# Two-layer adaLN transformer in fp32: the stage between the two attentions is reordered, batch by batch

## The chip, the core and the metric

The kernel runs on one NeuronCore of a Trainium2 chip. The metric is the device time of one execution in microseconds (us). A core has five engines that each work through their own instruction stream in order and meet only at semaphores: TensorE (PE in the profile), VectorE (DVE), ScalarE (ACT), GpSimd (POOL), and SyncE (SP), which here issues all DMA transfers. TensorE writes to eight PSUM banks of 128 x 512 fp32; the other engines read them.

## What is computed

The input `x` is 2 batches of 512 rows of 512 columns, here 8 tiles of 128 rows, 4 for each batch. Cut to what matters, the reference is:

```
mod = (silu(c) @ wmod).reshape(2, 6, 1, 512)          # per layer: sa, ca, ga, sb, cb, gb
ga, gb = (2*(g >= 0) - 1) * maximum(abs(g), 0.25)      # clamped gates
x = x + ga * attention(layernorm(x) * (1 + ca) + sa)
x = x + gb * feed_forward(layernorm(x) * (1 + cb) + sb)
# layer 0: attention with 32 query heads, 8 key/value heads, window 128
#          feed-forward = h @ W.T + bias + sum_e w_e (h @ A_e.T) @ Bf_e.T
# layer 1: attention with latents: c_q = h @ Wq_down, c_kv = h @ Wkv_down (64 wide),
#          128 heads of 4 content columns and 64 rotary columns; then a mixture of LoRA experts
```

## The kernel before, in words

Products are made from split operands: a value is held as `_hi` plus `_lo` (both fp32r), and a group `mm3` of three matmuls per pair, `hi*hi + hi*lo + lo*hi`, stands for one fp32 product. Nothing is scheduled by a program: the order of each engine is the order in which its block of the source is written, and a wait holds everything behind it on that engine.

*Layer 0's attention* runs over 8 key/value heads (`kv_head`), each in two halves, one for each batch; a half has 4 slots, one for each block of 128 queries (`slot` 0 to 63; the last half is slots 60 to 63, batch 1 of head 7). In a slot, TensorE makes `scores`, DVE masks and reduces them (`mask`), ACT takes exponentials (`exps`), DVE divides (`normalise`), TensorE transposes (`transposes`) and multiplies with the values (`sum_values`), ACT and DVE split the result (`out_high`, `out_low`), and `project_out` adds the slot's share of the output, which `gate_attention` (DVE) gates and `add_attention` (POOL) adds to `x`. In all but the last half, TensorE fills the waits with the projections of the next half (`more` in the code).

*Between the attentions* stand, before the change all behind the last slot: the merge of layer 0's feed-forward weights (`merge(k)`: W.T plus the LoRA product, 4 groups of 6 fp32 matmuls, from transposed `fbfT` and scaled `fa_s`, split by `merged_high` on ACT and `merged_low` on DVE); layer 1's modulation (`mod(1, c)` for 6 chunks, `mod_use` turns each chunk's rows into columns or gate sums, `mod_cols`, `clamp_gates`, `broadcast_gate`); the second norm of layer 0 (`norm_stats`, `norm_rows` on DVE, transposes `norm` on TensorE, scale and shift on ACT into `full`, split into `hT_hi` and `hT_lo` by DVE and POOL in `norm_split` and `norm`); the feed-forward (`ffn(t)` for 8 tiles); the first norm of layer 1 (phase 2 of the same functions); and layer 1's latent stages: `latent` (both down-projections), the rotary keys (`kr_mm`, copied by ACT to `k1` and `km`, whose unused rows POOL has zeroed), `content(0)`, and the value columns `vc`. In the latent stages before, each function loops over both batches.

*Layer 1's attention* runs over 128 units (64 head pairs by 2 batches) in `period(u, ...)`. A period makes the scores of unit u, the row maxima of unit u+2 and the rotary queries of unit u+3 (`rope_queries`), so the first three periods (u = -3 to -1) only fill the pipeline, with `content(1)` to `content(3)` between them. The content parts go to DRAM and come back by DMA (`store_content`, then `km` and `q2`).

## Time and profile before

| | us |
|---|---|
| timed, 3 runs, median (lowest to highest) | 2375.38 (2375.05 to 2375.47) |
| profiled execution, its own time | 2367.75 |
| its span, first to last instruction | 2365.9 |
| mean granted TensorE clock over the span | 0.98 of full |

The profiled execution was 7.6 us shorter than the median of the timed ones. The table's span counts from the first instruction; every time of day in the rows is counted from there. The stage at stake lies between 719.68 (the last half of the first attention begins) and 898.14 (the scores of unit 0 of the second one).

### The profile page before, as it was taken

The page shows a single profiled execution, that of the slowest core. Times are in us where ns is not written, and L with a number is a line of the kernel's source. Part 1 is how long each engine was busy: PE and PEld are TensorE (multiplying, and loading weights), DVE is VectorE, ACT ScalarE, POOL GpSimd, SP SyncE. Part 2 cuts the span into 40 slices and gives each one's busy share as a digit, 9 for nine tenths or more (in the row PEclk, how much of TensorE's full clock was granted, in tenths as well). Part 3 has the DMA queues.
Part 4 walks back from the last instruction along what each step waited for, and adds up shares of the span by engine and source line. Part 5 has one row for each costly group of instructions (what it writes and reads, how often), then busy time and mean ns, then how long its engine had stood idle before and what let it go on. Part 6 is the DMA issues. An engine that isn't in the chain of part 4 may idle for free.

```text
span 2365.9 us, 40739 instructions
## 1 busy us (share of the span) xinstructions
PE 2254.3 (95%) x11084; PEld 1676.5 (71%) x11084; DVE 1661.0 (70%) x3066; ACT 1346.5 (57%) x2633; POOL 587.4 (25%) x428
## 2 busy tenths in 40 slices
PE   6999999999998879999999999999999999999968
PEld 4788888888885546777777777777777777776646
DVE  6677777787775557767676676767767676767746
ACT  2444444444543246767767676677767677676721
POOL 4455655655651320000000000000000000002322
PEclk9999999999998979999999999999999999999988
DMA  5101010100022132111111111111111111113330
GB/s 190 57 28 45 18 44 27 43 19 27 18 66 89 28 118 91 39 39 38 38 35 39 38 38 34 38 40 37 39 33 39 39 38 38 35 40 90 94 108 36
DMA packets 117151, 117.49 MB, mean 50 GB/s; under 512 B 28925, under 2 KB 71453, under 8 KB 117100
## 3 DMA queue, kind: packets, MB, share of 16 engines
q1 hardware_dynamic: 117100, 116.85, 16.4%
q8 instruction: 27, 0.44, 0.1%
q14 instruction: 24, 0.20, 0.0%
HBM read 95.30 MB, written 20.97 MB: 49 GB/s over the span
## 4 chain that ended last, share of the span: by engine, by line
PE 87%; DVE 7%; issue 2%; SPq 1%; DMA 1%; ACT 1%; POOL 1%; POOLq 0%; DVEq 0%; ACTq 0%
PE bank L1830 11%; PE bank L1817 11%; PE bank L1831 10%; PE bank L1842 10%; PE bank L1530 8%; PE bank L1532 8%; PE bank L1531 8%; PE bank L1805 5%; PE bank L1803 5%; PE bank L1804 5%; PE bank L1618 1%; DVE probs L1198 1%; DMA wm<-in_L_wmod 1%; DVE rope_b L1177 1%; DVE rope_a L1175 1%
## 5 line engine op out<-in xcount | busy, mean ns | idle before, releaser
L1379 DVE TENSOR_REDUCE mcol<-bank 128x1 fp32r<-128x512 f32 x1024 | 694.6, 689 | 375.6 <-PE bank L1817 370.2
L1817 PE MATMUL bank<-km,q 128*128 128x512 f32 x1024 | 422.2, 413 | 12.0 <-DVE mcol L1379 7.3
L1830 PE MATMUL bank<-q,k 128*128 128x512 f32 x1024 | 419.9, 410 | 6.7 <-DVE c_lo L1350 3.3
L1831 PE MATMUL bank<-q,k 128*128 128x512 f32 x1024 | 405.4, 396 | 0.0
L724 POOL TENSOR_TENSOR wr_lo<-wst,wr_hi 128x512 fp32r<-128x512 f32 x64 | 81.7, 1277 | 1231.5 <-DVE wr_hi L1338 1231.5
L1817 PEld LDWEIGHTS bank<-km,q 128*128 128x128 f32 x1024 | 316.9, 310 | 78.1 <-issue 20.9
L1019 ACT ACTIVATE x<-bank 128x512 f32<-128x512 f32 x512 | 285.3, 601 | 91.1 <-PE bank L1831 86.6
L1019 ACT ACTIVATE pT<-bank 128x512 f32<-128x512 f32 x512 | 285.1, 600 | 87.0 <-PE bank L1831 83.4
L1830 PEld LDWEIGHTS bank<-q,k 128*128 128x128 f32 x1024 | 195.6, 191 | 134.2 <-issue 117.9
L1831 PEld LDWEIGHTS bank<-q,k 128*128 128x128 f32 x1024 | 192.6, 188 | 37.0
L1805 PE MATMUL bank<-hT_hi,wr_lo 128*128 128x512 f32 x512 | 206.7, 404 | 0.0
L1803 PE MATMUL bank<-hT_hi,wr_hi 128*128 128x512 f32 x512 | 204.4, 399 | 0.7 <-ACT vc L984 0.7
L1804 PE MATMUL bank<-hT_lo,wr_hi 128*128 128x512 f32 x512 | 203.5, 397 | 0.0
L1015 ACT ACTIVATE ost<-bank 128x512 f32<-128x512 f32 x128 | 76.5, 598 | 182.7 <-PE bank L1842 182.7
L1530 PE MATMUL bank<-hT_hi,w_hi 128*128 128x512 f32 x384 | 156.9, 409 | 16.7 <-DVE rope_b L1177 10.1
L845 ACT ACTIVATE probs<-probs,nmax 128x256 f32<-128x256 f32 (+1 forms) x256 | 120.1, 471 | 76.3 <-DVE nmax L1187 76.3
L1532 PE MATMUL bank<-hT_hi,w_lo 128*128 128x512 f32 x384 | 153.4, 400 | 0.0
L1531 PE MATMUL bank<-hT_lo,w_hi 128*128 128x512 f32 x384 | 152.9, 398 | 0.0
L852 ACT ACTIVATE pT_hi<-bank 128x512 fp32r<-128x512 f32 x112 | 61.8, 596 | 142.4 <-PE bank L1618 142.4
L620 POOL TENSOR_TENSOR rope_a<-rope_a,rope_b 128x512 f32<-128x512 f32 x80 | 103.0, 1288 | 124.2 <-DVE rope_b L1177 124.2
L1842 PE MATMUL bank<-x,vp 128*32 128x512 f32 x1024 | 124.1, 603 | 0.0
L1842 PE MATMUL bank<-pT,vp 128*32 128x512 f32 x1024 | 123.1, 598 | 0.8 <-ACT pT L1019 0.8
(270 smaller groups left out, 4133.1 us busy)
## 6 DMA issues: line engine op xcount, KB each, us to landing
wst<-in_L_attn_Wq_rope SPq DMA_DIRECT2D x64, 256.0 KB, 3.0
wm<-in_L_wmod SPq DMA_DIRECT2D x12, 1024.0 KB, 8.3
st_q<-in_L_attn_wq SPq DMA_DIRECT2D x8, 1024.0 KB, 6.1
st_wo<-in_L_attn_wo SPq DMA_DIRECT2D x8, 1024.0 KB, 5.1
km<-kc_d SPq DMA_DIRECT2D x256, 32.0 KB
q<-qc_d SPq DMA_DIRECT2D x256, 32.0 KB
k<-kc_d SPq DMA_DIRECT2D x256, 32.0 KB
o_d<-ost SPq DMA_DIRECT2D x512, 16.0 KB
```

The lines of the kernel that those rows point to most:

```text
L1019: act.activation(PT[k % 2][:, s], bank[s % 4][:], ACT.Exp, scale=float((HD1 + ROPE) ** -0.5)).then_inc(exp1, 1)
L1379: dve.tensor_reduce(mcol[:, k % 2, i % 4, i // 4:i // 4 + 1], bank[4 + i % 2][:], AX.X, ALU.max, negate=True)\
L1530: pe.matmul(ps, lh_, rh, start=(i == 0), stop=False)
L1531: pe.matmul(ps, lh_, rl, start=False, stop=False)
L1532: e = pe.matmul(ps, ll, rh, start=False, stop=(i == n - 1))
L1803: pe.matmul(bank[6][:], wr_hi[:, par, kk], hT_hi[:, kk, at], start=(kk == 0), stop=False)
L1804: pe.matmul(bank[6][:], wr_hi[:, par, kk], hT_lo[:, kk, at], start=False, stop=False)
L1805: e = pe.matmul(bank[6][:], wr_lo[:, par, kk], hT_hi[:, kk, at], start=False, stop=(kk == KT - 1))
L1817: pe.matmul(bank[4 + i % 2][:], q2[:, k % 4, h, i % 4:S:4], km[:, b, h], start=True, stop=True).then_inc(max_mm, 1)
L1830: pe.matmul(bank[s % 4][:], k1[:, k % 2, t], q1[:, k % 4, h], start=True, stop=False)
L1831: pe.matmul(bank[s % 4][:], k2[:, k % 2, h, t], q2[:, k % 4, h], start=False, stop=True).then_inc(scores1, 1)
L1842: e = pe.matmul(bank[7][32 * j:32 * j + 32, :], vp[:, k % 2, kb, h], PT[k % 2][:, s], start=(s < 4), stop=(s >= 4))
```

## The change

The merges, layer 1's modulation chunks 0 and 1, the broadcast of the feed-forward gate and the norm of batch 0 move into the last half of the first attention, between its slots, in the code of all engines (`merging`). Behind it, the feed-forward of batch 0 runs before the norm of batch 1 is turned; the norm of layer 1 and the latent stages are done for batch 0, then for batch 1. Banks 6 and 7, free in the last half, serve the merges, and the feed-forward then has these two banks instead of four. The buffers get other places so that nothing overlaps in time: `fa_s` is gone (`fa` is scaled in place), the chunks of `wmod` land in `wm_h`, `wm_l`, `wm1` and, after the merges, in `fw`. `rope_queries` of unit 0 and `content(1)` move ahead of the loop over periods, which starts at u = -2 on TensorE.

```diff
+            period(-3, 1)
+            store_content(0, (1,))
+            for i in range(2, 4):
+                sp.wait_ge(c_stored[i], 32)
+            store_content(1)
+            for u in range(-2, 0):
...
+            def add_ffn(t):
                 pool.wait_ge(f_gated, t + 1)
...
-            for b in range(B):
-                norm(2, b)
-
...
+            add_ffn(1)
+            norm(1, 1)
+            for t in range(2, 6):
+                add_ffn(t)
+            for i, (src, hi, lo) in enumerate(((dn, dn_hi, dn_lo), (kr, kr_hi, kr_lo))):
+                pool.wait_ge(pre_hi, i + 1)
+                pool.tensor_tensor(lo[:], src[:], hi[:].bitcast(F32), ALU.subtract).then_inc(pre_split, 1)
+            norm(2, 0)
+            add_ffn(6)
+            add_ffn(7)
+
+            pool.wait_ge(f_added, NT)
             pool.wait_ge(mod_mm, 12)
-            pool.memset(k2[:].bitcast(F32), 0.0).then_inc(zeroed, 1)
+            pool.wait_ge(mod_used, 12)
             pool.memset(km[:].bitcast(F32), 0.0).then_inc(zeroed, 1)
             pool.memset(q2[:].bitcast(F32), 0.0).then_inc(zeroed, 1)
+            pool.memset(k2[:].bitcast(F32), 0.0).then_inc(zeroed, 1)
+            pool.memset(ost[0:1, 0], 1.0).then_inc(zeroed, 1)
             pool.memset(vp[:], 0.0).then_inc(zeroed, 1)
             pool.memset(mcol[:].bitcast(F32), 0.0).then_inc(zeroed, 1)
-            wait_norm(pool, 2, 1)
-            pool.memset(ost[0:1, 0], 1.0).then_inc(zeroed, 1)
             pool.wait_ge(zeroed, 6)
             pool.memset(vp[:, :, :, :, HD1:2 * HD1], 1.0).then_inc(zeroed, 1)
+            norm(2, 1)
...
+                    if merging:
+                        merged_turned(0)
+                        merged_turned(1)
...
+                    if merging:
+                        merged_high(0)
+                        merged_high(1)
...
+                    if merging:
+                        norm_std(1, 0)
+                        merged_high(2)
                     out_high(slot + 2)
+                    if merging:
+                        merged_high(3)
                     weights_high(slot + 3, 3)
                     if more:
                         rope_high(half + 1, "Q3", nb)
+                    if merging:
+                        gates(0, 1, gate_f0)
+                        mod_rows(1, (0, 1))
+                        norm(1, 0, (0, 1))
                     out_high(slot + 3)
+                    if merging:
+                        norm(1, 0, (2, 3))
...
+            norm_std(2, 0)
+            mod_rows(1, (3,))
+            norm(2, 0)
+            mod_rows(1, (4,))
...
+            latent(0)
+            norm_std(2, 1)
+            gates(1, 0, gate[:, 1])
+            act.wait_ge(zeroed, 6)
+            keys(0)
...
+            content_high(0, (0,))
+            gates(1, 1, gate[:, 2])
+            norm(2, 1)
+            value_columns(0)
+            latent(1)
+            keys(1)
+            content_high(0, (1,))
+            value_columns(1)
...
+                    if merging:
+                        merged_factors()
...
+                    if merging:
+                        merged_scaled()
...
+                    if merging:
+                        norm_stats(1, 0)
                     out_low(slot + 1)
...
                     mask(slot + 3, 3)
+                    if merging:
+                        merged_low(0)
+                        merged_low(1)
...
                     gate_attention(slot + 1, b)
+                    if merging:
+                        merged_low(2)
                     out_low(slot + 2)
-                    if last and b == 1:
-                        norm_stats(1, 0)
+                    if merging:
+                        merged_low(3)
+                        norm_rows(1, 0)
...
+                    if merging:
+                        mod_cols(1, 0)
                     out_low(slot + 3)
+                    if merging:
+                        norm_split(1, 0)
+                        norm_stats(1, 1, (0, 1))
...
+            norm_stats(1, 1, (2, 3))
+            dve.wait_ge(fbias_loaded, 16)
+            dve.wait_ge(gate_ready, 2)
+            ffn_out(0)
+            norm_rows(1, 1)
+            ffn_out(1)
+            norm_split(1, 1)
+            ffn_out(2)
+            ffn_out(3)
+            norm_stats(2, 0)
+            ffn_out(4)
+            norm_rows(2, 0)
+            ffn_out(5)
+            clamp_gates(1)
+            norm_split(2, 0)
+            ffn_out(6)
+            ffn_out(7)
+            mod_cols(1, 1)
             norm_stats(2, 1)
             norm_rows(2, 1)
-            norm_split(2, 0)
-            norm_split(2, 1)
...
+            def merge_turn():
+
+                pe.wait_ge(f_loaded, 16 * 9)
+                pe.wait_ge(proj_free, TURNS * B * HKV)
+                pe.wait_ge(f_cw, 1)
+                for t in range(2):
...
+            def merge(k):
+
+                if k == 0:
+                    pe.wait_ge(f_as, 2)
+                    pe.wait_ge(f_trs, 2)
+                wait(pe, f_split, k - 1)
+                ps = merge_bank(k)
...
+            def norm_pair(i):
+
+                if i == 0:
+                    pe.wait_ge(col_ready, 3)
+                else:
+                    pe.wait_ge(ln_full, NT + 2)
+                for t in range(TB):
+                    pe.wait_ge(ln_norm, NT + t + 1)
+                    for k in (2 * i, 2 * i + 1):
+                        e = pe.transpose(norm_bank(1, k)[:, t * P:(t + 1) * P], xn1[:, t, k * P:(k + 1) * P], ident[:])
+                e.then_inc(ln_trans, 2)
...
+                    merging = last and b == 1
+                    if merging:
+                        merge_turn()
...
                     sum_values(slot, half, b, 0)
+                    if merging:
+                        merge(0)
...
                     transposes(slot + 1, 1)
+                    if merging:
+                        merge(1)
...
                     transposes(slot + 2, 2)
+                    if merging:
+                        merge(2)
...
                     sum_values(slot + 2, half, b, 2)
+                    if merging:
+                        merge(3)
...
+                    if merging:
+                        pe.wait_ge(f_split, KT)
+                        broadcast_gate(0, 1)
                     project_out(slot + 2, n)
+                    if merging:
+                        pe.wait_ge(gate_ready, 2)
+                        mod(1, 0)
+                        mod(1, 1)
+                        mod_use_cols()
                     sum_values(slot + 3, half, b, 3)
+                    if merging:
+                        norm_pair(0)
...
                     project_out(slot + 3, n)
+                    if merging:
+                        norm_pair(1)
...
                 at = slice(t * P, (t + 1) * P)
-                mm3(bank[4 + t % 4][:], [(hT_hi[:, k, at], hT_lo[:, k, at], fw_hi[:, k], fw_lo[:, k]) for k in range(KT)], f_mm)
...
             wait_norm(pe, 1, 0)
             ffn(0)
             ffn(1)
-            wait_norm(pe, 1, 1)
-            broadcast_gate(0, 1)
+            pe.wait_ge(wo_gated, NT * HKV)
+            mod(1, 2)
+            ffn(2)
+            norm(1, 1)
+            ffn(3)
+            mod(1, 5)
             mod_use(1, 2)
             mod_use(1, 5)
-            ffn(2)
-            ffn(3)
-            broadcast_gate(1, 0)
+            wait_norm(pe, 1, 1)
             ffn(4)
             ffn(5)
-            pe.wait_ge(gate_ready, 2)
-            broadcast_gate(1, 1)
+            mod(1, 3)
             ffn(6)
+            norm(2, 0)
             ffn(7)
-
-
-            pe.wait_ge(f_bias, NT)
-            norm(2, 0)
-            pe.wait_ge(gate_ready, 4)
-            norm(2, 1)
-            pe.wait_ge(pre_split, 2)
...
+            pe.wait_ge(pre_split, 2)
+            wait_norm(pe, 2, 0)
+            latent(0)
+            pe.wait_ge(f_bias, NT)
+            keys(0)
+            pe.wait_ge(col_ready, 4)
+            broadcast_gate(1, 0)
+            pe.wait_ge(lat_ready, 1)
+            content(0, (0,))
+            pe.wait_ge(gate_ready, 3)
+            broadcast_gate(1, 1)
+            pe.wait_ge(gate_ready, 4)
+            norm(2, 1)
+            pe.wait_ge(ln_full, 3 * NT)
+            value_columns(0)
+            pe.wait_ge(kr_split, 1)
+            rope_queries(0, 0, 0, range(KT), True, True)
+            wait_norm(pe, 2, 1)
+            latent(1)
+            keys(1)
+            pe.wait_ge(lat_ready, 2)
+            content(0, (1,))
+            value_columns(1)
+            pe.wait_ge(vc_ready, NT)
+            pe.wait_ge(kr_split, B)
+            content(1)
 
             def max_scores(w, k, i, use):
```

How the instructions stand now is shown at three places. The first is DVE in the last half, around slot 61's output: `probs`, `nmax` and `window` belong to `mask`, `oT` to `out_low`, `fw_lo` to `merged_low`. After the change:

```order
L1194 BN_STATS stats<-x 128x6 [waits attn0_added] x4
L1199 BN_AGGR mean_var<-stats 128x2 [waits ln_stats] x4
L1202 TENSOR_SCALAR var_eps<-mean_var 128x4 [waits ln_aggr]
L1284 TENSOR_TENSOR oT_lo<-bank,oT_hi 128x512 [waits oT_hi_done]
L1262 ISA probs,nmax<-bank,window 128x256 [waits scores0]
L1262 ISA nmax 128x1
...
L1262 ISA probs,nmax<-bank,window 128x256
L1262 ISA nmax 128x1
L1302 TENSOR_TENSOR fw_lo<-bank,fw_hi 128x512 [waits f_hi] x2
L1279 TENSOR_TENSOR pT_lo<-bank,pT_hi 128x512 [waits pT_hi_done]
```

The statistics of batch 0's norm stood behind slot 62's output before and stand ahead of slot 61's now, and the first two `fw_lo` stand behind them and behind slot 63's mask. The second place is GpSimd at the end of the stage, after the split of the second norm's odd columns (`hT_lo`); `MEMSET` zeroes the rows of the second attention's operands. Before, and then after:

```order
L701 TENSOR_TENSOR x<-x,fg 128x512 [waits f_gated] x6
L643 TENSOR_TENSOR hT_lo<-full,hT_hi 128x512 [waits ln_hi] x4
L711 MEMSET k 128x2048 [waits mod_mm,f_split]
L712 MEMSET km 128x2048
L713 MEMSET q 128x4096
L714 MEMSET vp 128x512
L715 MEMSET mcol 128x256
L717 MEMSET ost 1x512 [waits ln_lo_odd,ln_lo]
```

```order
L679 TENSOR_TENSOR hT_lo<-full,hT_hi 128x512 [waits ln_hi] x2
L736 TENSOR_TENSOR x<-x,fa 128x512 [waits f_gated] x2
L753 MEMSET km 128x2048 [waits mod_used,mod_mm,f_added]
L754 MEMSET q 128x4096
L755 MEMSET k 128x2048
...
L758 MEMSET mcol 128x256
L760 MEMSET vp 128x16x4 [waits zeroed]
L679 TENSOR_TENSOR hT_lo<-full,hT_hi 128x512 [waits ln_hi] x2
```

The zeroing moved ahead of batch 1's `hT_lo`, and now waits for the last addition of the feed-forward (`f_added`). The third place is ACT at the same time of the program; `gate` is the copy of a broadcast gate, `full` the scale and shift of a norm, `k` and `km` the rotary keys. Before:

```order
L821 ACTIVATE full<-bank,modc 128x512 [waits ln_trans,col_ready]
...
L821 ACTIVATE full<-bank,modc 128x512 [waits ln_lo,ln_trans,col_ready]
L821 ACTIVATE full<-bank,modc 128x512 [waits ln_lo_odd]
L821 ACTIVATE full<-bank,modc 128x512 [waits ln_lo]
L821 ACTIVATE full<-bank,modc 128x512 [waits ln_lo_odd]
L967 ACTIVATE lat<-bank 128x512 [waits lat_mm] x2
L971 ACTIVATE k<-bank 128x512 [waits kr_mm,zeroed]
L972 ACTIVATE km<-bank 64x512
L973 ACTIVATE km<-bank 64x512
L971 ACTIVATE k<-bank 128x512 [waits kr_mm]
```

After:

```order
L1026 ACTIVATE lat<-bank 128x512 [waits lat_mm]
L854 ACTIVATE std<-var_eps 128x4 [waits ln_eps]
L849 ACTIVATE gate<-bank 128x512 [waits gate_bc]
L849 ACTIVATE gate<-bank 128x512
L1031 ACTIVATE k<-bank 128x512 [waits kr_mm,zeroed]
L1032 ACTIVATE km<-bank 64x512
L1033 ACTIVATE km<-bank 64x512
L1050 ACTIVATE c_hi<-bank 128x512 [waits c_mm] x2
L849 ACTIVATE gate<-bank 128x512 [waits gate_bc]
L849 ACTIVATE gate<-bank 128x512
L869 ACTIVATE full<-bank,modc 128x512 [waits ln_lo,ln_trans,col_ready]
L869 ACTIVATE full<-bank,modc 128x512 [waits ln_lo_odd]
```

Batch 1's four `full` stand behind the keys, which wait for the zeroing, and behind the last gate copy.

## Rows read from the trace of the kernel before

**Rows 1.** The page: busy time, share of the span and instructions of TensorE.

```profile
PE 2254.3 (95%) x11084; PEld 1676.5 (71%) x11084; DVE 1661.0 (70%) x3066; ACT 1346.5 (57%) x2633; POOL 587.4 (25%) x428
```

**Rows 2.** Windows: us, busy of PE, PEld, DVE, ACT, POOL, then PEclk, DMA, GB/s.

```profile
719.68:789.16 69.48, 57.19 (x306) 40.43 (x305) 36.99 (x92) 23.10 (x54) 9.08 (x7) 0.90 0.23 70
789.16:821.13 31.97, 31.23 (x115) 20.53 (x113) 21.91 (x35) 7.17 (x13) 14.82 (x11) 0.95 0.00 1
821.13:869.38 48.25, 37.28 (x125) 23.07 (x125) 22.43 (x42) 18.72 (x33) 16.50 (x14) 0.82 0.24 91
869.38:898.14 28.76, 18.85 (x56) 12.68 (x57) 22.77 (x39) 11.61 (x20) 1.27 (x1) 0.82 0.49 180
719.68:753.83 34.15, 27.21 (x136) 21.25 (x135) 21.80 (x54) 12.11 (x35) 5.14 (x4) 0.95 0.00 1
```

**Rows 3.** TensorE in order of time: start, us, line, what, [idle before <-releaser].

```profile
768.75 1.88 PE L1710 MATMUL bank<-fbfT,fa_s 128*128 128x512 f32 x4
...
771.45 1.07 PE L1542 MATMUL bank<-wm,silu 128*32 128x512 f32 x8
772.45 1.05 PE L1555 MATMUL bank<-rowsum,modrow 128*128 128x2 f32 x8
...
787.44 1.97 PE L1571 MATMUL bank<-ident,xn 128*128 128x128 f32 x16 [1.41 <-DVE fw_lo L1302]
...
795.66 1.95 PE L1563 MATMUL bank<-grows,sel 32*128 32x512 f32 x4 [0.73 <-issue]
797.54 1.74 PE L1551 MATMUL bank<-modrow,rowsum 128*32 128x512 f32 x4
```

**Rows 4.** Groups of DVE in 719.68 to 900: busy us, mean ns, idle before.

```profile
L1147 DVE TENSOR_TENSOR hT_lo<-full,hT_hi 128x512 fp32r<-128x512 f32 x8 | 10.4, 1300 | 0.3
...
L1119 DVE BATCH_NORM_STATS2 stats<-x 128x6 f32<-128x512 f32 x16 | 9.8, 676 | 0.0
...
L1321 DVE TENSOR_TENSOR fg<-xn,gate 128x512 f32<-128x512 f32 x8 | 7.1, 884 | 4.2 <-ACT gate L805 4.0
L1144 DVE CAST hT_hi<-full 128x512 fp32r<-128x512 f32 x16 | 6.3, 419 | 7.5 <-ACT full L821 7.5
...
L1198 DVE TENSOR_TENSOR probs<-probs,rden 128x1024 f32<-128x1024 f32 x3 | 4.8, 1593 | 0.1
...
L1187 DVE CUSTOM_DVE_ANT_0 probs<-bank,window 128x256 f32<-128x256 f32 x12 | 4.3, 417 | 0.2 <-PE bank L1532 0.2
...
L1104 DVE TENSOR_SCALAR gsign<-gsign 64x512 f32<-64x512 f32 x1 | 1.0, 1022 | 0.0
```

**Rows 5.** Groups of ACT in the same stretch.

```profile
L821 ACT ACTIVATE full<-bank,modc 128x512 f32<-128x512 f32 x16 | 11.2, 775 | 10.2 <-PE bank L1571 9.4 <-POOL hT_lo L643 0.9
L979 ACT ACTIVATE c_hi<-bank 128x512 fp32r<-128x512 f32 x16 | 8.3, 603 | 0.4 <-PE bank L1782 0.3
L845 ACT ACTIVATE probs<-probs,nmax 128x256 f32<-128x256 f32 x12 | 5.9, 500 | 2.5 <-DVE nmax L1187 2.5
```

**Rows 6.** GpSimd in order of time around the zeroing.

```profile
824.27 1.27 POOL L701 TENSOR_TENSOR x<-x,fg 128x512 f32<-128x512 f32 x1 [3.06 <-DVE fg L1321]
...
839.41 1.80 POOL L711 MEMSET k<- 128x2048 f32 x1
...
847.10 0.52 POOL L717 MEMSET ost<- 1x512 f32 x1
```

**Rows 7.** TensorE in order of time behind the feed-forward.

```profile
828.24 3.43 PE L1571 MATMUL bank<-ident,xn 128*128 128x128 f32 x16 [2.75 <-DVE xn L1136]
834.85 0.47 PE L1530 MATMUL bank<-hT_hi,dn_hi 128*128 128x512 f32 x1 [3.19 <-POOL hT_lo L643]
...
850.00 1.88 PE L1789 MATMUL bank<-vup,lat 64*128 64x512 f32 x4
853.65 8.71 PE L1789 MATMUL bank<-vup,lat 64*128 64x512 f32 x12 [1.77 <-ACT vc L984]
```

**Rows 8.** TensorE where unit 0 begins.

```profile
898.14 0.50 PE L1830 MATMUL bank<-q,k 128*128 128x512 f32 x1 [3.27 <-DVE c_lo L1350]
```

352 lines of the change are left out of this document (166 added, 186 removed).

## The prediction

> **What bounds the kernel now.** I read the page first: TensorE is busy 95% of the span [rows 1]. So the question is where its 5% idle lies, and the windows answer it. From the last half of the first attention to the end of the weight merges and of batch 0's turning, TensorE works 57.19 of 69.48 us; the feed-forward is nearly gapless (31.23 of 31.97); the next 48.25 us hold 37.28 of work at a clock of 0.82, and the 28.76 before unit 0 only 18.85 [rows 2]. I call these stretches A, B, C and D. Behind 898.14, where unit 0 begins [rows 8], the loop is the same in both kernels and TensorE-bound, so a shift at unit 0 stays to the end. The sum below is therefore: the four stretches after, against 178.46 us before. In order of time I then read what TensorE waits for: DVE's `fw_lo` ahead of batch 0's turning (1.41) [rows 3], GpSimd's `hT_lo` ahead of the latents (3.19), ACT's `vc` between value columns (1.77) [rows 7], `c_lo` ahead of unit 0 (3.27) [rows 8]. No stretch is held by a transfer. What a change here can win is thus about 32 us of idle time (12.3, 0.7, 11.0 and 9.9) and the half-clock stretches; what it can lose is any wait that it puts on TensorE's stream in place of those.
>
> **A: the last half takes the merges in.** Work, at the full clock. The last half itself: 27.2, the last row of [rows 2]. Turning `fbf` (8 transposes, half of the 1.97 of 16) and the expansion: 1.6. Four merges at 2.7 each, the distance of 768.75 to 771.45: 10.8. The gate's broadcast 1.95. Two modulation chunks at 0.98: 1.9. Their two column groups: 2.1. Batch 0's turning 1.97 [rows 3]. Sum 47.5.
>
> New waits. They come from one fact: merges, statistics and softmax now stand in one line on each engine.
> (a) The factors for the scale stand behind slot 61's mask (four pieces of 0.42 with their readouts of 0.08, from 1.9 us of mask, of which 0.2 is covered) [rows 4]: 1.8.
> (b) Their turned copy stands behind slot 61's division of 1.59, which itself waits for ACT's exponentials, 4 x 0.5 with readouts [rows 4, 5]: 2.9.
> (c) Merge 0 waits for the two copies of `fbfT` behind ACT's `oT_hi`, each 0.6, as `c_hi` of the same shape [rows 5]: 1.9.
> (d) Merge 2 needs the bank of merge 0, so `fw_lo` of merge 0. On DVE that stands behind the division (1.59), four statistics (4 x 0.68, with small ones 3.0), `oT_lo` (0.6), and slot 63's mask (4 x 0.42, with the readouts 1.9) [rows 4]; TensorE has slot 61's projection, slot 62's transposes and the next scores to lay against it. Left: 4.5.
> (e) Small ones at slot 63's transposes, the gate's broadcast and the modulation row: 0.7, 0.7, 0.9.
> (f) The last projection waits for `oT_hi`, which on ACT stands behind two `full` of 0.78 [rows 5], then `oT_lo` 0.7 on DVE: 3.0.
> (g) The first feed-forward tile waits for the second pair of `full` (1.6), DVE's `hT_hi` and GpSimd's `hT_lo` (1.3 to 1.4, as its addition of the same size, 1.27 [rows 6]): 3.7.
> Sum 20.1. The clock falls in two of these waits; before, the whole of A stood at 0.90 [rows 2], and I put 2.6 more for matmuls at half speed. A: 47.5 + 20.1 + 2.6 = 70.2, against 69.5. The last half hides nothing of what moves in, since TensorE was not idle there: 27.2 of 34.15 is work, and the moved work of 20.3 is 2.9 times the idle 6.9 that it could fill.
>
> **B: the feed-forward.** Before: 31.97 less three broadcasts (5.9), the gate sums (1.74) and the wait of 0.73 [rows 2, 3] leaves 23.6 for 8 tiles. After, with three chunks of 0.98 to 1.0 (3.0), the gate sums (1.7) and two turnings (3.9): 32.2. Banks: only two for eight tiles, each freed by DVE's sum behind statistics (0.68 each) and casts (0.42 each) [rows 4]: 1.3, an estimate for two short waits. B = 33.5.
>
> **C: the latents batch by batch.** Here the change loses. Piece by piece after the last feed-forward tile:
> 1. Last chunk, its row, two column groups, then the wait for batch 0's `hT_lo` (1.3 to 1.4 on GpSimd, behind ACT's `full` and DVE's cast); DVE has `clamp_gates` ahead of that split, four passes of which one takes 1.02 [rows 4], some 3.3: 7.5.
> 2. `latent(0)` and `keys(0)`: 24 matmuls, as many as two feed-forward tiles (5.9), part at half clock: 7.7.
> 3. Broadcast and content pair 3.1 (1.95 [rows 3], and a pair of the size of the value columns' 0.94 [rows 7]); broadcast of the last gate, of which one half is slow: 2.7.
> 4. **The wait on which the change turns.** TensorE's `norm(2, 1)` takes batch 1's banks after the last gate copy on ACT. That copy stands behind `keys(0)`, which waits for all zeroing; and GpSimd's zeroing now waits for the feed-forward's last addition. From the last tile's end: DVE still has `clamp_gates` 3.3, `hT`'s four casts (0.42) and two splits (1.30), 4.3, then the last two tiles' sums (0.7) and gatings (0.88), 3.1: 10.7, of which 0.5 lies before; the addition 1.27; zeroing 8.2 (839.41 to 847.6); keys 1.7, content 1.0 and gate 1.0 on ACT [rows 4 to 6]. That is 23.4, and 24.2 with 0.8 for five handovers from engine to engine, an estimate; items 1 to 3 end at 21.0. Wait: 3.2.
> 5. Turning at half clock, 3.9 (3.43 at 828.24 [rows 7], with its first one's latency).
> 6. Four `full` on ACT before the first value column may take its bank, 4 x 0.78 less the first's overlap: 2.9.
> 7. Four value columns at 1.7 each, half clock: 6.9.
> 8. `rope_queries(0)` 4.9, partly at half clock.
> 9. `latent(1)`, `keys(1)`: 5.6. Content pair 1.0.
> 10. Four value columns of batch 1, 5.3, a wait 0.7, `content(1)` 4.2 (four at 0.47 of work [rows 7], the rest ACT's `c_hi` copies at 0.6 [rows 5] that free the banks).
> C = 7.5 + 7.7 + 3.1 + 2.7 + 3.2 + 3.9 + 2.9 + 6.9 + 4.9 + 5.6 + 1.0 + 5.3 + 0.7 + 4.2 = 59.6, against 48.25. Of the 11.4 more, 3.1 is chunk and column work that came from A, 3.9 are two broadcasts that came from B, and the rest is slow matmuls; the idle time of before (11.0) is not won, it stands at other places.
>
> The price of item 7 is open from both sides. At the full clock two columns (four records) took 1.88, or 0.94 each; partly at half speed six (twelve records) took 8.71, or 1.45 each, and all at half speed one would take 1.9 [rows 7]. So four cost 3.8 at least and 7.5 at most. I take 6.9, near the upper end, because TensorE has just waited twice before them, as it had before the six. The trace shows a half-speed turning (3.43 for 16 against 1.97), and the matmul at 834.85, with nothing but that turning and a wait before it, took 0.47, so the clock had come back up in or behind it [rows 7]. The Trainium skill's "TensorE: Matmul & The Clock Gate", section "Part 4: PE-mode transpose", says that transposes don't raise the clock as other matmuls do. This trace speaks against it. By the page the columns behind the turning run at half speed, as I priced them; by the row they may run at full speed, 3.1 us cheaper in all.
>
> **D.** Before, 28.76 with 18.85 of work: two waits for maxima, one for `c_lo` (3.27) [rows 2, 8]. After, `q` and the first content parts were split earlier, since both stand ahead of the loop: 2.0 less of waits and 1.8 less of half clock. D = 25.0.
>
> **Sum.** 70.2 + 33.5 + 59.6 + 25.0 = 188.3, less 178.5 = +9.8. The profiled execution's own time was 2367.75, so 2377.6. The median of the runs lies 7.6 above the profiled one; the same distance gives **2385.2**, or +0.41%. A measurement tells some 0.2%, 4.75 us, from no change.
>
> **The rivals.**
> *Same, 2373 to 2380.* The clock stays up in C: item 7 falls from 6.9 to 3.8, item 5 from 3.9 to 2.0 [rows 3, 7], which makes 5.0; items 2 and 8 may lose 1 to 2 each and A its 2.6, up to 12 in all. For it: the 0.47 at 834.85. Against: every idle stretch of C before was followed by slow ones (0.82 [rows 2]). Chance 0.14.
> *Faster, 2368 to 2371.* The last half's waits (a) to (e), 13.4 in all, don't arise, since DVE reaches the factors, the statistics and `fw_lo` in time; with 2.6 of clock, 9.8 - 16.0 = -6.2, so 2369.2. It decides when A's waits fall under 5.5. For it: DVE was busy only 21.8 of 34.15 us there [rows 2]. Against: the order on DVE is fixed, and masks wait for scores that stand behind the merge. Chance 0.11.
> *Slower still, 2391 to 2393.* The merges run at half clock in A (each would be 1.9 longer, as 3.43 is to 1.97 [rows 3, 7]) or the chain of item 4 grows, because DVE's `xn` of batch 1 and GpSimd's zeroing delay each other: +6 to +8. Chance 0.14.
> *Forecast, 2380 to 2391.* Chance 0.61.
>
> **How the numbers follow.** Faster by over 0.2% (under 2370.6) is 0.11. Same (to 2380.1) takes the clock's case and a little of the forecast's lower edge: 0.15. Slower: 0.74. The range 2374 to 2393 leaves out the faster case and parts of the outer two.
>
> **What would show it.** In the changed kernel's trace: merge 2 idle about 4.5 before its first matmul, released by `fw_lo`; the last `wo` product idle 3 for `oT_lo`; the first feed-forward matmul at about 789.9; the feed-forward ending near 823.4; the transposes of `norm(2, 1)` waiting on the last gate's copy, with GpSimd's zeroing from 11.5 to 20 us behind the last tile; unit 0's first scores at about 908. It is wrong if the zeroing ends early enough for the keys not to wait, if A comes out under 64 us, or if the feed-forward shows gaps of a tile's length for its two banks.

## The result and the profile after

The changed kernel takes 2379.87 us (median of 20 runs, 2373.30 to 2385.07) against 2372.98 of the kernel before (20 runs, 2359.87 to 2377.14). The ratio is 1.0032 with a 95% interval of 1.0021 to 1.0044: slower by 5 to 10 us (the medians differ by 6.9). The profiled execution's own time is 2378.89, its span 2377.1, its mean granted clock 0.976. Two executions of the kernel of experiment 10 took 2784.52 and 5776.39 us, far from all others; the ratios leave them out.

The page, busy time of the engines, against [rows 1]:

```profile
PE 2261.0 (95%) x11084; PEld 1678.5 (71%) x11084; DVE 1666.9 (70%) x3066; ACT 1348.9 (57%) x2633; POOL 588.0 (25%) x428
```

The number of instructions is the same on every engine, and TensorE is busy 6.7 us longer with them: that is clock, not work. The four stretches (from, to, length, busy time of PE, PEld, DVE, ACT and POOL, then PEclk), against [rows 2]:

```profile
721.33:790.93 69.60, 50.91 (x247) 36.23 (x245) 31.96 (x78) 22.05 (x51) 7.72 (x6) 0.88 0.05 15
790.93:824.27 33.34, 32.63 (x156) 23.05 (x156) 26.69 (x49) 8.55 (x15) 13.52 (x11) 0.95 0.30 91
824.27:883.00 58.73, 47.34 (x142) 26.99 (x141) 30.54 (x46) 19.21 (x35) 20.14 (x15) 0.72 0.23 83
883.00:909.33 26.33, 18.16 (x59) 11.84 (x57) 21.02 (x36) 11.25 (x19) 1.27 (x1) 0.85 0.54 196
```

A is 69.6 (before 69.5), B 33.3 (32.0), C 58.7 (48.3), D 26.3 (28.8); together 188.0 against 178.46. From unit 0's first scores to the end both kernels take the same 1467.8 us (2377.1 less 909.33, 2365.9 less 898.14). The shift does stay to the end. The other 1.65 us between the two spans lie ahead of the last half, where both kernels run the same work.

TensorE in A, in order of time:

```profile
725.22 0.57 PE L1744 MATMUL bank<-fcw,expand 16*128 16x1 f32 x4 [1.87 <-DVE fcw L1290]
...
728.71 1.12 PE L1750 MATMUL bank<-ident,fbf 128*128 128x128 f32 x4 [2.34 <-DVE fer L1295]
...
732.87 3.75 PE L1761 MATMUL bank<-fbfT,fa 128*128 128x512 f32 x4 [1.76 <-ACT fbfT L986]
...
739.97 1.88 PE L1761 MATMUL bank<-fbfT,fa 128*128 128x512 f32 x4
...
754.18 3.68 PE L1761 MATMUL bank<-fbfT,fa 128*128 128x512 f32 x4 [4.34 <-DVE fw_lo L1302]
...
781.57 0.80 PE L1631 MATMUL bank<-wo_hi,oT_hi 128*128 128x512 f32 x1 [2.81 <-DVE oT_lo L1284]
...
790.93 0.47 PE L1631 MATMUL bank<-fw_hi,hT_hi 128*128 128x512 f32 x1 [3.91 <-POOL hT_lo L679]
```

There stand the forecast waits (a), (b), (c), (d), (f) and (g): 1.87, 2.34, 1.76, 4.34, 2.81 and 3.91. The reader is to see a second thing in the second column: the first four matmuls of merges 0 and 2, each behind such a wait, took 3.75 and 3.68, and those of merge 1, with work ahead of it, 1.88. A wait can be paid twice, once as idle time and once as slow matmuls behind it.

TensorE in C and D:

```profile
830.85 0.76 PE L1631 MATMUL bank<-hT_hi,dn_hi 128*128 128x512 f32 x1 [2.77 <-POOL hT_lo L679]
...
847.74 3.67 PE L1674 MATMUL bank<-ident,xn 128*128 128x128 f32 x16 [3.60 <-ACT gate L849]
854.34 7.19 PE L1921 MATMUL bank<-vup,lat 64*128 64x512 f32 x8 [2.92 <-ACT full L869]
...
886.00 0.62 PE L1974 MATMUL bank<-km,q 128*128 128x512 f32 x1 [1.84 <-DVE mcol L1480]
...
909.33 0.50 PE L1987 MATMUL bank<-q,k 128*128 128x512 f32 x1 [3.27 <-DVE c_lo L1445]
```

And the engines that it waits for, GpSimd's zeroing, DVE's `xn` and ACT's copies:

```profile
834.57 1.80 POOL L753 MEMSET km<- 128x2048 f32 x1
...
843.95 0.32 POOL L760 MEMSET vp<- 128x64 f32 x1
```

```profile
837.26 6.38 DVE L1211 TENSOR_SCALAR xn<-x,mean_var,rstd 128x512 f32<-128x512 f32 x4
```

```profile
841.03 1.09 ACT L849 ACTIVATE gate<-bank 128x512 f32<-128x512 f32 x2 [4.01 <-PE bank L1666]
843.92 0.60 ACT L1031 ACTIVATE k<-bank 128x512 fp32r<-128x512 f32 x1 [1.81 <-POOL mcol L758]
...
846.59 1.09 ACT L849 ACTIVATE gate<-bank 128x512 f32<-128x512 f32 x2
851.50 2.78 ACT L869 ACTIVATE full<-bank,modc 128x512 f32<-128x512 f32 x4 [3.82 <-issue]
```

The keys' copies on ACT wait 1.81 for the zeroing (`mcol` is the last memset that they need), the last gate's copy ends at 847.7, and batch 1's turning starts with it. Four value columns at half clock take 7.19.

### The profile page after: what moved, and what is told of

Read it like the earlier page. It is cut to its first block, busy times and chain, and to the rows that moved or that the text cites. A ratio compares the mean times of both kernels' runs of the same rounds, so it can differ in the third digit from the quotient of the medians.

```text
span 2377.1 us, 40741 instructions
## 1 busy us (share of the span) xinstructions
PE 2261.0 (95%) x11084; PEld 1678.5 (71%) x11084; DVE 1666.9 (70%) x3066; ACT 1348.9 (57%) x2633; POOL 588.0 (25%) x428
## 4 chain that ended last, share of the span: by engine, by line
PE 58%; DVE 2%; SPq 1%; DMA 1%; issue 1%; ACT 1%; POOL 0%; POOLq 0%; DVEq 0%; ACTq 0%
PE bank L1987 11%; PE bank L1974 10%; PE bank L1988 10%; PE bank L1999 10%; PE bank L1935 5%; PE bank L1933 5%; PE bank L1934 5%; PE bank L1921 0%; DMA dnm<-o_d 0%; SPq L582 0%; SPq L624 0%; PE bank L2125 0%; PE bank L2127 0%; PE bank L2126 0%; DVE c_lo L1445 0%
```

## The experiments

The measure is the stretch from the last half's first transposes to unit 0's first scores (178.46 before, 188.0 after), with its parts A to D, each from one profiled execution, and the ratio of the timed runs (6 to 12 of each kernel, one each in 11 and 12) to runs of the kernel before in the same session. Small differences in the stretches need care: C, with the same order in it, took 58.7 in the changed kernel and in run 5, and 56.1 and 56.4 in runs 4 and 6.

**1. The merges behind the last half again.** On each engine the calls of the `merging` branches move behind `kv_head(HKV - 1, True)`, except batch 0's statistics and what follows from them on DVE and ACT, which stay in the last half (the statistics still ahead of slot 61's output); for TensorE:

```diff
-                    if merging:
-                        merge(0)
...
             kv_head(HKV - 1, True)
+            merge_turn()
+            for k in range(KT):
+                merge(k)
+            pe.wait_ge(f_split, KT)
+            broadcast_gate(0, 1)
+            pe.wait_ge(gate_ready, 2)
+            mod(1, 0)
+            mod(1, 1)
+            mod_use_cols()
+            norm_pair(0)
+            norm_pair(1)
```

> This kernel is the changed one with its merges, factors, gate broadcast, first two modulation chunks and batch 0's turning put back behind the last half on every engine; the batch-by-batch order behind them stays. The stretch from the last half's first transposes to unit 0's first scores (178.5 us before, 188.0 in the changed kernel) is the measure. Theory 1 (the loss is in the latent stages, the interleaving hides little because TensorE was not idle there): 190 to 195, so 2 to 7 us slower than the changed kernel, and 11 to 16 slower than the kernel before. Rival (the new waits inside the last half eat more than the interleaving hides): 183 to 187, faster than the changed kernel.

Measured: 2382.43 us, ratio 1.0047 (1.0029 to 1.0064). A and the whole stretch (722.96 to 911.84, 188.9 us):

```profile
722.96:793.17 70.21, 50.90 (x247) 35.32 (x245) 34.32 (x84) 22.37 (x51) 8.96 (x7) 0.89 0.11 28
722.96:911.84 188.88, 149.55 (x598) 97.71 (x596) 111.19 (x206) 61.50 (x119) 42.32 (x32) 0.84 0.22 75
```

A is 70.2, against 69.6 with the interleaving. Taking the work into the last half returned 0.6 us in the profile. Both theories are missed, each by a little: it isn't faster without the waits, and it isn't 2 to 7 slower either. Within 1 us the interleaving hid as much as its waits cost; the intervals of the timed ratios, 1.0029 to 1.0064 here and 1.0021 to 1.0044 for the changed kernel, overlap.

**2. The latent stages in the old order.** Broadcasts, `norm(2, 1)`, both latents, both keys, contents and value columns, and on GpSimd the zeroing behind batch 1's split; for TensorE:

```diff
             pe.wait_ge(pre_split, 2)
-            wait_norm(pe, 2, 0)
-            latent(0)
-            pe.wait_ge(f_bias, NT)
-            keys(0)
             pe.wait_ge(col_ready, 4)
             broadcast_gate(1, 0)
-            pe.wait_ge(lat_ready, 1)
-            content(0, (0,))
             pe.wait_ge(gate_ready, 3)
             broadcast_gate(1, 1)
             pe.wait_ge(gate_ready, 4)
             norm(2, 1)
-            pe.wait_ge(ln_full, 3 * NT)
-            value_columns(0)
-            pe.wait_ge(kr_split, 1)
-            rope_queries(0, 0, 0, range(KT), True, True)
+            wait_norm(pe, 2, 0)
+            latent(0)
             wait_norm(pe, 2, 1)
             latent(1)
+            pe.wait_ge(f_bias, NT)
+            keys(0)
             keys(1)
             pe.wait_ge(lat_ready, 2)
-            content(0, (1,))
+            content(0)
+            value_columns(0)
             value_columns(1)
             pe.wait_ge(vc_ready, NT)
             pe.wait_ge(kr_split, B)
+            rope_queries(0, 0, 0, range(KT), True, True)
             content(1)
```

> The changed kernel with the latent stages in the old order again (both gate broadcasts, batch 1's turning, both latents, both batches' keys, contents and value columns; zeroing behind batch 1's split); the last half and the feed-forward stay changed. If the batch-by-batch latent stage as such is what costs (theory 1 as the forecast put it, C 59 instead of 48), the stretch falls to 180 to 184. Rival: what costs is that broadcasts and modulation work stand behind the last feed-forward tile in either order, and batch 0's work ahead of batch 1's hides part of batch 1's chain; then it stays at 188 to 192.

Measured: 2382.52, ratio 1.0048 (1.0032 to 1.0065); the stretch is 188.7. C and D:

```profile
823.79:879.75 55.96, 42.76 (x140) 24.96 (x141) 23.45 (x43) 18.71 (x35) 18.61 (x15) 0.79 0.24 86
879.75:908.70 28.95, 19.04 (x58) 12.80 (x56) 22.84 (x39) 11.82 (x21) 1.27 (x1) 0.80 0.50 182
```

C falls to 56.0, D rises to 28.95, and nothing is won: the rival's number holds. In net the batch order is worth nothing here in either direction; it isn't free of waits in either, since with the old order TensorE idles 5.30 us ahead of the first broadcast, where `latent(0)` and `keys(0)` stand in the changed kernel:

```profile
832.74 3.75 PE L1664 MATMUL bank<-grows,sel 32*128 32x512 f32 x4 [5.30 <-issue]
```

By elimination, what C and D have more than before is the work that the change put behind the last feed-forward tile, and the waits and slow matmuls around it; no run takes that work away by itself.

**3. The last gate later.**

```diff
             pe.wait_ge(gate_ready, 3)
-            broadcast_gate(1, 1)
-            pe.wait_ge(gate_ready, 4)
             norm(2, 1)
...
             pe.wait_ge(kr_split, B)
+            broadcast_gate(1, 1)
             content(1)
+            pe.wait_ge(gate_ready, 4)
```

> The last gate's broadcast and copy stand behind the value columns of batch 1 instead of ahead of batch 1's turning; nothing else moves. Theory 1: the 3.60 us wait for that gate's copy goes, and with it the broadcast's 2 us from that place, of which 1 to 2 come back at the new place; the next to end late is the division of batch 1's rows on DVE (843.6), so the turning starts some 4 us earlier and the stretch is 184 to 186. Rival (the clock): the same idle time moves to other places and stays at half clock; 187 to 189.

Measured: 2382.96, ratio 1.0037 (1.0019 to 1.0054); the stretch is 186.55, between the two expectations.

```profile
845.55 2.03 PE L1674 MATMUL bank<-ident,xn 128*128 128x128 f32 x16
852.66 7.19 PE L1921 MATMUL bank<-vup,lat 64*128 64x512 f32 x8 [5.08 <-ACT full L869]
...
876.19 2.78 PE L1666 MATMUL bank<-grows,sel 32*128 32x512 f32 x4 [0.69 <-ACT vc L1039]
```

The 3.60 us wait is gone, and the next one on the same chain grew from 2.92 to 5.08, since ACT's `full` stand behind the keys, which stand behind the zeroing. The broadcast costs 2.78 at its new place. 1.5 us of 3.6 remain in the profile, and the timed runs don't show them; run 7 doesn't confirm them.

**4. to 6. DVE's order in the last half.** Two edits, alone and together:

```diff
+                    if merging:
+                        merged_factors()
                     mask(slot + 1, 1)
                     if merging:
-                        merged_factors()
+                        merged_scaled()
...
-                    if merging:
-                        merged_scaled()
                     mask(slot + 2, 2)
...
                     normalise(slot + 2, 2)
-                    if merging:
-                        norm_stats(1, 0)
...
                         merged_low(0)
                         merged_low(1)
+                        norm_stats(1, 0)
```

The first, the factors early:

> Only DVE's order in the last half changes: the merge's factors ahead of slot 61's mask, their scaling ahead of slot 61's division. In the kernel with both orders and the late gate stretch A fell from 69.9 to 60.3. Theory (each late operation on DVE costs on its own, so the gains add): the waits for the factors (1.87) and for their turned copy (2.34) go and A is 65 to 67. Rival (it was one chain, and a gain shows only when the statistics move as well): A stays at 68 to 70 and the 4.34 us wait for the first low part grows.

Measured: 2372.82, ratio 1.0007 (0.9996 to 1.0018). The second, the statistics late:

> Only batch 0's statistics (3.0 us of DVE) move behind the first two low parts of the merged weights. Theory: the wait of 4.34 for the first low part falls to about 1.5 and A is 65 to 67. Rival: A stays at 68 to 70, since slots' masks and divisions follow the same chain.

Measured: 2377.64, ratio 1.0023 (1.0011 to 1.0035). Both:

> Both DVE orders, the gate as in the changed kernel. Theory (the waits in the last half are what the change lost): A is 60 to 61 and the stretch to unit 0 is 178 to 179, against 188.0: as fast as the kernel before within 0.2%, ratio 0.999 to 1.003. Rival (the late gate gave part of it): the stretch is 181 or more and the ratio 1.003 or more.

Measured: 2371.11, ratio 0.9993 (0.9978 to 1.0009); stretch 178.0. A of the three:

```profile
725.19:788.51 63.32, 47.78 (x246) 34.50 (x245) 32.14 (x78) 21.93 (x51) 7.70 (x6) 0.95 0.05 17
```

```profile
723.23:790.18 66.95, 51.13 (x247) 37.03 (x245) 31.86 (x78) 21.82 (x51) 7.71 (x6) 0.87 0.05 16
```

```profile
723.37:785.55 62.18, 49.50 (x247) 36.28 (x245) 32.03 (x78) 21.69 (x51) 7.69 (x6) 0.88 0.05 17
```

A is 63.3, 67.0 and 62.2, against 69.6: savings of 6.3, 2.6 and 7.4 (run 4 did better than its 65 to 67, run 5 as its theory had it, run 6 missed its 60 to 61 by 1 but met 178 to 179 for the stretch). With the factors early the waits in front of them are 0.4 and 0.2 instead of 1.87 and 2.34, and merge 0 runs at the full clock. TensorE in run 6, with both edits:

```profile
725.78 0.57 PE L1743 MATMUL bank<-fcw,expand 16*128 16x1 f32 x4 [0.41 <-DVE fcw L1290]
...
727.17 0.65 PE L1749 MATMUL bank<-ident,fbf 128*128 128x128 f32 x4 [0.22 <-DVE fer L1295]
...
730.74 1.96 PE L1760 MATMUL bank<-fbfT,fa 128*128 128x512 f32 x4 [2.22 <-ACT fbfT L986]
...
747.07 1.98 PE L1760 MATMUL bank<-fbfT,fa 128*128 128x512 f32 x4 [1.48 <-DVE fw_lo L1302]
```

The first three rows of run 4 are the same within 0.02 us. Its 6.3 us come between A's start and merge 1: half is idle time (3.1: the two waits less 3.6, the wait for `fbfT` more by 0.5), half is slow matmuls (3.2; the granted clock there is 1.00, and 0.70 to 0.74 in the changed kernel). The statistics alone shorten (d) from 4.34 to 1.49, and 2.6 come out: here only the idle time. Merge 2 runs at the full clock, but the slow matmuls come back 13 us later, as "What the runs showed of the hardware" shows for run 6.

Two edits of DVE's order, in which no work changes, take back all that the change lost: the ratio falls from 1.0032 (1.0021 to 1.0044) to 0.9993 (0.9978 to 1.0009). Of the 10.0 us in the stretch 7.4 are A's; the other 2.6 come out of B to D, where nothing was edited, and are clock or chance. The timed runs don't separate run 4 from run 6, nor run 5 from the changed kernel: those intervals overlap.

**7. Both DVE orders and the late gate.** The edits of 3 and 6 together.

> The gate as in the kernel with the late gate; besides, in the last half DVE makes the merge's factors ahead of slot 61's mask and scales them ahead of slot 61's division, and takes batch 0's statistics behind the first two low parts of the merged weights. Theory: the waits of 1.87, 2.34 and 4.34 us in the last half go, but masks and divisions get later by 2 to 3; with the late gate the stretch is 180 to 184 and the time 2 to 6 us under the changed kernel. Rival: each wait removed comes back as another one of the same length in this one-line order; 184 to 187.

Measured: 2373.62, ratio 1.0000 (0.9985 to 1.0016); stretch 176.65, A 60.3. The stretch is 1.3 us under run 6, but that isn't the late gate: A is 1.9 shorter though all of its order is the same (the granted clock in it is 0.94 here and 0.88 there), and B to D, where the gate moved, are 0.5 longer. Single executions differ by that much. The late gate shows no gain, here or in the timed runs. The stretch is under both expectations.

**8. Four banks for batch 0's turning.** On top of 7, ACT splits slot 63's output ahead of the scale and shift, and the turning doesn't wait for banks:

```diff
             if ph == 1 and j < KT:
-                return bank[6 + j % 2]
+                return bank[(0, 1, 6, 7)[j]]
...
-                if i == 0:
+                if i == 1:
                     pe.wait_ge(col_ready, 3)
-                else:
-                    pe.wait_ge(ln_full, NT + 2)
...
                     if merging:
                         norm_pair(0)
+                        norm_pair(1)
                     project_out(slot + 3, n)
-                    if merging:
-                        norm_pair(1)
...
                         mod_rows(1, (0, 1))
-                        norm(1, 0, (0, 1))
                     out_high(slot + 3)
                     if merging:
-                        norm(1, 0, (2, 3))
+                        norm(1, 0)
```

> Besides both DVE orders and the late gate: batch 0's turning takes four banks (0, 1, 6, 7) in one go ahead of the last projection, and ACT splits the last slot's output ahead of the scale and shift. It takes away the waits of 2.81 us (last projection) and 3.9 us (first feed-forward tile). Theory: both shrink, to 1 and 2; A is 55 to 58 and the ratio to the kernel before 0.997 to 0.999. Rival: the scale and shift end later because they stand behind the output, so the first tile waits longer: A 59 to 61, no change to the kernel with 60.3.

Measured: **2358.19 us, ratio 0.9949 (0.9929 to 0.9969)**, faster than both kernels. Its stretches:

```profile
717.40:771.94 54.54, 45.87 (x246) 33.24 (x245) 33.12 (x78) 21.80 (x51) 7.83 (x6) 0.97 0.06 20
771.94:805.34 33.40, 32.69 (x160) 23.10 (x164) 26.85 (x50) 8.70 (x15) 13.65 (x11) 0.95 0.29 91
805.34:860.09 54.75, 44.98 (x141) 24.43 (x141) 29.69 (x44) 19.17 (x35) 19.68 (x15) 0.79 0.25 90
860.09:885.80 25.71, 16.77 (x59) 11.13 (x57) 21.98 (x38) 11.25 (x19) 1.27 (x1) 0.93 0.55 201
```

A is 54.5, the whole 168.4. The wait of 2.81 ahead of the last projection is gone, that of the first tile is 2.69 instead of 3.9. The theory's mechanism holds and was priced too low: A came out under 55 and the ratio under 0.997, since half clock went with the waits (PEclk 0.97 in A). Of the gain over run 7, 5.8 us are A's, where the edit is, and 2.5 are D's, where nothing was edited. The rest of the timed gain (15 us between the medians of 7 and 8, against 8.3 in the stretch) is not located: the two profiled executions differ by 6.9 us outside the stretch, over the same work.

**9. Rotary queries ahead of the value columns**, on top of 8:

```diff
+            pe.wait_ge(kr_split, 1)
+            rope_queries(0, 0, 0, range(KT), True, True)
             pe.wait_ge(ln_full, 3 * NT)
             value_columns(0)
-            pe.wait_ge(kr_split, 1)
-            rope_queries(0, 0, 0, range(KT), True, True)
```

> The fastest version so far (both DVE orders, late gate, four banks for batch 0's turning) with one more move: unit 0's rotary queries (12 matmuls of 512 columns) ahead of batch 0's value columns instead of behind them, into the wait of 4.54 us for the scale and shift. Theory: the wait goes and C falls from 54.8 to 50 to 52, ratio to before 0.992 to 0.994. Rival: the value columns' copies then come later on ACT and the queries' matmuls run at half clock (5.1 us), so that C falls by under 1.

Measured: 2366.56, ratio 0.9978 (0.9965 to 0.9991): 7 to 8 us worse than 8, a miss of both. The row says why:

```profile
826.82 2.63 PE L1672 MATMUL bank<-ident,xn 128*128 128x128 f32 x16
839.94 0.77 PE L1928 MATMUL bank<-hT_hi,wr_hi 128*128 128x512 f32 x1 [10.49 <-POOL wr_lo L766]
```

The queries need `wr_lo`, and on GpSimd that stands behind batch 1's `hT_lo`. I had looked at the banks and the keys, not at the third operand. A wait of 4.5 turned into one of 10.49, and C rose from 54.8 to 57.8 instead of falling.

**10. The zeroing of the keys' rows first**, in the changed kernel:

```diff
             pool.memset(km[:].bitcast(F32), 0.0).then_inc(zeroed, 1)
+            pool.memset(k2[:].bitcast(F32), 0.0).then_inc(zeroed, 1)
             pool.memset(q2[:].bitcast(F32), 0.0).then_inc(zeroed, 1)
-            pool.memset(k2[:].bitcast(F32), 0.0).then_inc(zeroed, 1)
...
-            act.wait_ge(zeroed, 6)
+            act.wait_ge(zeroed, 2)
             keys(0)
...
+            act.wait_ge(zeroed, 7)
```

> The changed kernel with the rotary keys' rows zeroed first (1.8 and 2.1 us) and ACT waiting for these two alone; nothing else moves. In the changed kernel the keys' copy on ACT waited 1.81 us for the zeroing, and the last gate's copy stands behind it. The forecast's item 4 (the zeroing sets the turning's start): the wait before batch 1's turning falls from 3.6 to 1.8 and C by 1.8 at least. Rival (the first gate's copy and the broadcasts set it, not the zeroing): C stays within 0.5 us of 58.6.

Measured: 2380.16, ratio 1.0025 (1.0010 to 1.0041). C and D:

```profile
828.05:881.31 53.26, 43.85 (x142) 25.62 (x141) 28.68 (x44) 18.63 (x35) 19.89 (x15) 0.78 0.25 92
881.31:909.66 28.35, 18.77 (x58) 12.46 (x57) 22.53 (x38) 11.46 (x20) 1.27 (x1) 0.82 0.50 182
```

```profile
849.48 3.08 PE L1675 MATMUL bank<-ident,xn 128*128 128x128 f32 x16 [1.67 <-ACT gate L849]
```

The wait falls from 3.60 to 1.67, as item 4 said. C falls by 5.5, of which D gives 2.0 back. What is beyond the 1.9 of the wait is mostly clock (0.78 against 0.72 in C, 0.82 against 0.85 in D), and the timed runs can't tell the result from the changed kernel's.

**11. and 12. The wait filled.** In the changed kernel TensorE does work that nobody reads, into a free bank, in its wait ahead of batch 0's value columns: six matmuls, or twelve transposes.

```diff
+            pe.wait_ge(kr_split, 1)
+            for i in range(6):
+                pe.matmul(bank[6][:], hT_hi[:, i % KT, 0:P], hT_hi[:, i % KT, 0:S], start=True, stop=True)
             pe.wait_ge(ln_full, 3 * NT)
             value_columns(0)
```

```diff
+            pe.wait_ge(kr_split, 1)
+            for i in range(12):
+                pe.transpose(bank[6][:, (i % KT) * P:(i % KT + 1) * P], xn1[:, i % TB, 0:P], ident[:])
```

> The changed kernel with six matmuls of 512 columns whose result nobody reads, in TensorE's wait of 2.92 us ahead of batch 0's value columns. They change no result and remove no work. If the half clock behind the wait (7.19 us for four columns, then 12 matmuls at half clock until 866.7) comes from TensorE's idling, the columns take 4 to 6 and unit 0's queries 3 to 4, so C falls by 2 to 5. Rival (the clock is down for another reason than idle time): C stays at 58.6 or grows by the filling that overruns the wait.

> The same wait filled with twelve transposes of 128 columns instead, about as long. If transposes hold TensorE's clock as other matmuls do, C comes out as with the six matmuls. If they don't count, the four value columns stay at 7.2 and C at 58.6.

Measured, one run each: 2377.38 and 2377.01. TensorE around the filled wait, with matmuls and then with transposes:

```profile
849.15 3.68 PE L1674 MATMUL bank<-ident,xn 128*128 128x128 f32 x16 [3.44 <-ACT gate L849]
852.48 2.75 PE L1954 MATMUL bank<-hT_hi 128*128 128x512 f32 x6
855.76 3.79 PE L1921 MATMUL bank<-vup,lat 64*128 64x512 f32 x8 [0.53 <-ACT full L869]
```

```profile
849.05 3.67 PE L1674 MATMUL bank<-ident,xn 128*128 128x128 f32 x16 [3.46 <-ACT gate L849]
852.52 2.60 PE L1954 MATMUL bank<-ident,xn 128*128 128x128 f32 x12
855.66 3.79 PE L1921 MATMUL bank<-vup,lat 64*128 64x512 f32 x8 [0.53 <-ACT full L869]
```

The value columns fall from 7.19 to 3.79 in both, and C from 58.7 to 52.5, more than expected; D gives 1.4 back, and the whole stretch is 183.3 in both, 4.7 under the changed kernel's. No work was removed and nothing started earlier: `full` was as late as before. The turning and the filling itself still ran at about half clock (3.67 for 16 transposes, 2.60 for 12, against 1.97 for 16 at the full one), and the clock was back by the value columns; with the wait left empty it stayed down until 866.7. The half clock behind the wait was TensorE's own idling. One timed run each, inside the changed kernel's 2373.30 to 2385.07, can't say whether the 4.7 us are won in time.

## Why the prediction was right, and where its sizes were off

The forecast was +9.8 us for the profiled execution, 2385.2 for the median, slower with 0.74. The stretch came out at +9.5, the median at 2379.87, the ratio at 1.0032 where +0.41% stood. The order of the four stretches, and what each does, hold; the median's rise is 2.9 us smaller than the forecast. I can't attribute that part to a term: the single executions of one kernel spread over 12 to 17 us, the profiled ones of all fourteen kernels reach the last half between 717.4 and 725.2 us with the same work behind them, and the runs' median of the kernel before moved by 2.4 with more runs. The forecast's +0.41% lies inside the measured interval, 0.21 to 0.44%. That +9.8 comes so close to +9.5, a sum of dozens of terms against one execution each, is in part luck; that the timed kernel is slower is not. One slip in the forecast's text changes nothing in its sum: the idle time of before in A to D (12.3, 0.7, 11.0, 9.9) is 33.9, not about 32.

**A** (70.2 forecast, 69.6 measured). The waits (a) to (d), 1.8, 2.9, 1.9 and 4.5, measured 1.87, 2.34, 1.76 and 4.34; (e) 0.40, 0.54 and 0.72 for 0.7, 0.7 and 0.9; (f) and (g) 2.81 and 3.91 for 3.0 and 3.7. Together they are 18.7 of idle time for 20.1. The rival "faster" put the turning point at 5.5 us of waits left, with 2.6 of clock on top of the idle time. Run 6 bears that out: (a) to (e) are down from 12.0 to 6.0, and the stretch is back at the kernel before's (178.0 against 178.46). The 6.0 of idle time brought 10.0 in the stretch, so the clock's share came out at 4.0 in the stretch, of which 1.4 in A, for the forecast's 2.6. The edits of run 8 together bring 19.6 (168.4). The rival's mechanism was real; in the order as it was written it didn't come about.

**B** (33.5, measured 33.3). Two banks in place of four cost nothing that shows: the only wait is 0.71, for `hT_lo`.

**C** (59.6, measured 58.7). Item 4's chain ran as told: zeroing 834.57 to 844.3, keys, content, last gate, and a wait of 3.60 for 3.2. The zeroing started 10.1 us behind the last tile's end, not 11.5, and took 9.3 up to the memset that the keys wait for, instead of 8.2. That GpSimd's zeroing and DVE's `xn` delay each other stood in the rival "slower still": it came about (`xn` 6.38 us instead of 1.92), but only the 1.1 us of the zeroing lay on the chain. Items 6 and 7 are 2.92 and 7.19 for 2.9 and 6.9. But "the wait on which the change turns" is too large a word: run 3 removed it and 1.5 us came out of the profile and nothing out of the timed runs, run 10 halved it with no timed gain, and run 2, without the batch order, is no faster. C is 10.5 us longer. Idle time is 0.4 of that (11.4 against 11.0). The rest, 10.1, is busy time: 7.0 of chunk, column and broadcast work moved in (3.1 and 3.9, as forecast), 2.0 of batch 0's turning moved out to B (the forecast's account of C's growth left that out, its sum did not), and so some 5 of slow matmuls. Run 11 puts a size on what the clock costs behind the one wait of 2.92: 6 us in C. The forecast's rival "same" had 3.1 for item 7 and 1 to 2 for item 8; run 11 gave 3.4 and 2.4. So its prices were nearly right, but its condition, a clock that stays up, never came about in the changed kernel.

**D** (25.0, measured 26.3). It is 2.4 shorter than before instead of 3.8: the first wait for maxima is down from 3.58 to 1.84, but the second (3.06) and the one for `c_lo` (3.27, as in [rows 8]) stayed.

**The transposes.** The Trainium skill's "TensorE: Matmul & The Clock Gate", section "Part 4: PE-mode transpose", has transposes not count as busy for the clock the way other matmuls do. The forecast set one row of before against it, 0.47 at 834.85. The rows behind that one show how thin it was:

```profile
835.16 0.49 PE L1531 MATMUL bank<-hT_lo,dn_hi 128*128 128x512 f32 x1
835.45 0.63 PE L1532 MATMUL bank<-hT_hi,dn_lo 128*128 128x512 f32 x1
```

The clock was up for two matmuls and then down for seven, so the first row behind a wait doesn't tell the price. Run 12 settles it for this place: from 849.05 to 855.1 TensorE did nothing but transposes, and the eight matmuls behind them took 3.79, exactly as with six matmuls in the wait, against 7.19 with it empty. Here the rule does not hold. The price of item 7 was nevertheless right, because the wait stood behind the turning.

Still open is what the batch order would be worth in a version without waits in C: run 8 still has 54.75 there, with waits of 2.75 and 4.54 in it. Between run 1 and run 4, A falls by 6.9 and the timed ratio from 1.0047 (1.0029 to 1.0064) to 1.0007 (0.9996 to 1.0018): with the factors early the interleaving pays. It isn't shown whether the merges behind the last half would gain from DVE's other order too.

## What to carry to other kernels

Work moved into an attention's slots pays by the place that it takes in the line of the engine that feeds TensorE, not by the idle time of TensorE that it could fill: here the merge's factors (a product of 16 numbers) behind a mask, and statistics ahead of a split, cost that stage 7.4 us and the whole stretch up to 10. Put what releases TensorE first and what is due later (statistics) behind it. In run 8 four banks for a turning, together with the last output ahead of the scale and shift on ACT, brought another 5.8 in A; which of the two did it wasn't separated. Price each wait with the slow matmuls that may follow it, and before work is moved ahead, follow all of its operands, the low halves too.

## What the runs showed of the hardware

An empty wait of 2.92 us was followed by 7.19 us for eight matmuls; with matmuls or transposes in it, the same eight took 3.79.

The slow matmuls don't always stand directly behind the wait, and a wait doesn't always cost them. Runs 6 and 8 have the same wait of 1.48 ahead of merge 2. Run 6 (its merge 2 is shown above, 1.98) and then run 8, each with a matmul of the projection behind the gate's broadcast:

```profile
760.52 0.63 PE L1631 MATMUL bank<-wo_lo,oT_hi 128*128 128x512 f32 x1
```

```profile
741.08 3.65 PE L1759 MATMUL bank<-fbfT,fa 128*128 128x512 f32 x4 [1.48 <-DVE fw_lo L1301]
...
756.07 0.39 PE L1630 MATMUL bank<-wo_lo,oT_hi 128*128 128x512 f32 x1
```

Run 8 pays at merge 2: from there to merge 3 takes 8.6 us, and 6.9 in run 6. Run 6 pays behind the broadcast: from there to the modulation row takes 9.1 us, and 7.5 in run 8. The price is 1.6 to 1.7 us in either, 13 us apart in place. In run 4 merge 0 stands behind 2.21 us of idle time and still takes 1.95. What decides where the clock falls, these runs don't show; so a single row behind a wait is no measure of its cost, and the stretch around it is.

DVE's four `xn` of batch 1 took 6.38 us in the changed kernel, from 837.26 on, while GpSimd zeroed from 834.57 to 844.3; in the kernel before the same four took 1.92, from 827.54 on, with GpSimd idle. In run 10 they took 6.36 beside the zeroing, but in run 4, with the same order around them, 3.54, so the size isn't fixed. It was hidden here by the wait for the gate.
